# Decoder layer with a routed feed-forward: gate logits of batch 0 before the last out-projection, two copies out of PSUM dropped, fewer spare products, and another order at the end of cross-attention

## What is computed

```python
x = x + xattn(layernorm(x), ctx, bias, mask)      # 16 heads, softmax over the context
x = x + attn(layernorm(x))                        # 16 heads, values clamped
x = x + ffn(layernorm(x))

def ffn(x, gate_w, w1, w2):                       # x: 4 batches, 128 rows, 512 columns
    k = int(2.0 * t / 8)                          # 32 rows for each expert of each batch
    scores = jnp.einsum('ntd,de->nte', x, gate_w)
    probs = jax.nn.softmax(scores, axis=-1)
    probs = jnp.transpose(probs, (0, 2, 1))
    g, m = jax.lax.top_k(probs, k)
    xin = jax.vmap(lambda xb, mb: xb[mb])(x, m)
    h = jax.nn.gelu(jnp.einsum('nekd,edf->nekf', xin, w1))
    h = jnp.einsum('nekf,efd->nekd', h, w2)
    weighted = g[..., None] * h                   # added back to the rows that were chosen
```

## Time and profile before

| | |
|---|---|
| median of 3 runs | 452.39 us |
| lowest and highest | 452.37 and 452.97 us |
| the profiled execution's own time | 454.42 us |
| its span, first to last instruction | 452.7 us |
| mean granted clock of PE | 0.990 |
| PE busy | 440.6 us, 97% |
| DVE busy | 367.3 us, 81% |
| ACT busy | 302.2 us, 67% |
| share of PE in the chain that ended last | 89% |
| share of DVE in it | 6% |

### The profile page before, as it was taken

One profiled execution on the slowest core, in us unless ns is written; L12 is line 12 of the kernel. 1 busy time (PEld: TensorE's weight loads), 2 busy tenths in 40 slices (PEclk: granted clock), 3 DMA queues, 4 the chain that ended last, 5 costly groups with the idle time before them and its releaser, 6 DMA issues.

```text
span 452.7 us, 9864 instructions
## 1 busy us (share of the span) xinstructions
PE 440.6 (97%) x3428; PEld 365.8 (81%) x3428; DVE 367.3 (81%) x516; ACT 302.2 (67%) x622; POOL 87.0 (19%) x111
## 2 busy tenths in 40 slices
PE   8999999999998999999999999999999999999995
PEld 3888888888887789878888787878788787878795
DVE  6889777777779876668978989888989898998972
ACT  4637666666666643667274878787777878777852
POOL 7100000000000122000133250505041230505002
PEclk9999999999999999999979999999999999999999
DMA  7980000000000921800000499999999999998002
GB/s 263 381 295 26 25 23 23 23 23 23 23 26 21 340 89 66 262 19 3 1 0 1 168 387 386 385 387 387 385 332 350 351 307 349 312 376 304 28 1 93
DMA packets 43105, 82.02 MB, mean 181 GB/s; under 512 B 2632, under 2 KB 3784, under 8 KB 43080
## 3 DMA queue, kind: packets, MB, share of 16 engines
q1 hardware_dynamic: 41816, 81.09, 51.0%
q10 hardware_dynamic: 1264, 0.59, 0.5%
HBM read 80.57 MB, written 1.10 MB: 180 GB/s over the span
## 4 chain that ended last, share of the span: by engine, by line
PE 89%; DVE 6%; DMA 1%; issue 1%; ACT 1%; DVEq 0%; POOL 0%; SPq 0%
PE po L1699 19%; PE pk L1699 11%; PE pv L1699 10%; PE pk L1306 8%; PE pv L1316 6%; PE ps L1335 5%; PE ps L1415 3%; PE pv L1335 3%; PE po L1725 3%; PE ps L1460 3%; PE po L1428 2%; PE ps L1408 2%; PE po L1335 2%; DMA x_s<-in_x 1%; PE pk L1335 1%
## 5 line engine op out<-in xcount | busy, mean ns | idle before, releaser
L1242 DVE TENSOR_TENSOR w_lo<-att_w,w_hi 128x2048 fp32r<-128x2048 f32 x60 | 138.0, 2309 | 21.3 <-ACT w_hi L705 21.3
L705 ACT CAST w_hi<-att_w 128x2048 fp32r<-128x2048 f32 x60 | 115.1, 1918 | 15.5 <-PE po L1699 15.5
L488 ACT ACTIVATE big_a<-ps,negm 128x128 f32<-128x128 f32 x176 | 62.2, 394 | 0.0
L1699 PE MATMUL po<-w_hi,ht_hi 128*128 128x512 f32 (+1 forms) x128 | 50.0, 391 | 0.0
L1699 PE MATMUL po<-w_hi,ht_lo 128*128 128x512 f32 (+1 forms) x128 | 48.6, 380 | 0.0
L1699 PE MATMUL po<-w_lo,ht_hi 128*128 128x512 f32 (+1 forms) x128 | 48.6, 380 | 0.0
L1306 PE MATMUL pk<-ctx_s,att_w 128*128 128x128 f32 x352 | 42.1, 278 | 0.0
L1306 PEld LDWEIGHTS pk<-ctx_s,att_w 128*128 128x128 f32 x352 | 40.2, 192 | 1.9 <-issue 1.8
L488 ACT ACTIVATION_READ_ACCUMULATOR big_a<-ps,negm 128x1 f32 x176 | 41.1, 233 | 0.0
L908 DVE TENSOR_REDUCE mc<-ps 128x8 f32<-128x1024 f32 x22 | 26.9, 1221 | 10.0 <-PE ps L1408 9.9
L1699 PEld LDWEIGHTS po<-w_hi,ht_lo 128*128 128x128 f32 x128 | 24.0, 188 | 5.0
(11 more groups left out here) (348 smaller groups left out, 1027.0 us busy)
## 6 DMA issues: line engine op xcount, KB each, us to landing
att_w<-in_w SPq DMA_DIRECT2D x64, 1024.0 KB, 7.2
ctx_s<-in_ctx_t SPq DMA_DIRECT2D x11, 256.0 KB, 2.7
x_s<-in_x SPq DMA_DIRECT2D x4, 256.0 KB, 4.0
att_w<-in_wk SPq DMA_DIRECT2D x1, 1024.0 KB, 8.0
att_w<-in_wq SPq DMA_DIRECT2D x1, 1024.0 KB, 10.4
att_w<-in_wv SPq DMA_DIRECT2D x1, 1024.0 KB, 11.9
att_w<-in_sv SPq DMA_DIRECT2D x1, 1024.0 KB, 14.6
att_w<-in_wo SPq DMA_DIRECT2D x1, 1024.0 KB, 14.8
```

What stands on the lines that cost most here:

```text
L488: ins = a.activation(big_a[:, h], ps[:, c, g * P:(g + 1) * P], ACT.Exp, bias=negm[:, h:h + 1], accum_out=sums[:, h:h + 1])
L705: a.copy(w_hi[:, i % SLOTS], att_w[:, i]).then_inc(hi_ok, 1)
L1242: v.tensor_tensor(w_lo[:, i % SLOTS], att_w[:, i], w_hi[:, i % SLOTS], ALU.subtract).then_inc(lo_ok, 1)
L1699: ins = mm(dst, l, r, start=start and i == 0, stop=i == len(terms) - 1, skip_group_check=True)
```

## The change

Three places in the gate and one in cross-attention:

- `gate_project(0)` moves from behind `turn_gate(2)` to ahead of `out_project(3)`.
- `keep_busy(5, 4)` becomes `keep_busy(3, 4)`.
- The first round of top-k reads the probabilities in `pv`; the copy to `prob_t` is gone. The comparison that makes `onehot` reads the slots in `pk`; the copy to `slot_t` is gone. Since the third group of the gather writes `pk`, PE waits for the second half of `onehot` ahead of it.
- In the step before the last chunk PE runs scores, `turn_batch(1, 0)`, `v_project(t + 1, 3)`, value product, instead of `v_project(t + 1, 3)`, scores, `turn_batch(1, 0)`, value product.

```diff
@@ vector engine, top-k
             dve.wait_ge(pt_g, 1)
-            link(v.tensor_copy(prob_t, pv[0:B * E, 0:T]))
-            src = prob_t
+            src = pv[0:B * E, 0:T]
             for r in range(CAP // 8):
...
             dve.wait_ge(slot_mm, 1)
-            link(v.tensor_copy(slot_t[:], pk[:, 0:B * E]))
...
-                v.tensor_tensor(onehot[:, now].rearrange("p b e s -> p (b e) s"), slot_t[:, rows].unsqueeze(2).broadcast_to([P, 2 * E, CAP]),
+                v.tensor_tensor(onehot[:, now].rearrange("p b e s -> p (b e) s"), pk[:, rows].unsqueeze(2).broadcast_to([P, 2 * E, CAP]),
@@ tensor engine, chunk
-                v_project(t + 1, 3)
-                scores(t + 1)
                 if at_end:
+                    scores(t + 1)
                     turn_batch(1, 0)
+                    v_project(t + 1, 3)
+                else:
+                    v_project(t + 1, 3)
+                    scores(t + 1)
                 values(t)
@@ tensor engine, gate
             out_project(2)
+            gate_project(0)
             out_project(3)
             turn_gate(1)
             turn_gate(2)
-            gate_project(0)
             turn_gate(3)
...
-            keep_busy(5, 4)
+            keep_busy(3, 4)
...
+                if c == 2:
+                    pe.wait_ge(onehot_ok, 2)
```

More of the change, by code:

```diff
@@ L93, in decoder_layer @@
         top8 = sb("top8", [B * E, 8])
-        slot_t = sb("slot_t", [P, B * E])
         iota_s = sb("iota_s", [P, CAP])
@@ L143, in decoder_layer @@
         rounded = sb("rounded", [P, B, D], BF16)
-        prob_t = ctx_s[0:B * E, 0]
         work = ctx_s[0:B * E, 1:3]
```

## The result

| | before | changed |
|---|---|---|
| median | 452.97 us (7 executions) | 455.53 us (7) |
| lowest and highest | 452.37 and 454.45 | 453.82 and 456.38 |
| ratio, with 95% interval | | 1.0043 (1.0028 to 1.0057) |
| profiled execution: own time, span | 454.42, 452.7 | 455.53, 453.8 |
| its mean granted clock | 0.990 | 0.990 |

The change makes the kernel slower by 0.43%, about 1.9 us (the means of the seven executions differ by 2.0, the medians by 2.6). The forecast was +0.2 us.

The account below looks back on a forecast made before the run. PE, busy for 97% of the span, was taken as the bound; cross-attention 0, gate to `onehot` +0.16 and PSUM reads +0.03 gave +0.19, so median 452.39 became 452.6 us, with range 451.2 to 453.3.

Parts of the forecast that it names:

- Cross-attention's end: Last value projection moved behind the scores: value product 0.70 later, absorbed by later waits; cost 0, bounds 0 and +0.7.
- Rival D: Cross-attention's end costs something: the 0.24 slack fails (453.2) or the clock drops there too (455); chance 0.05.
- The order in the gate: Batch 0's logits ahead of the last out-projection: batch 3's logits 0.43 later, bounds 0 and +0.79.
- Rival B: In the gate the clock does not fall, so `onehot` comes earlier: 451.4; chance 0.27.
- The step from there to `onehot`: Gate, batch 3's logits onward: half-rate logits +0.75, partly regained in the 15 spares, `onehot` +0.16; with PSUM reads +0.19.
- The copies: Top-k and slots in the gate read PSUM directly: three reads on DVE, taken +0.03, bounds 0 and 0.1.
- Without the copy 4.34: DVE from start of top-k to the end of batch 3's low part: 4.34 in place of 4.65.
- the 0.31: Time the probabilities' copy held back top-k's first round; its gain was forecast to be hidden by PE's spares.
- Taken +0.03: Forecast cost of three DVE reads from PSUM in the gate, +0.01 each; PE's new wait taken as 0.
- I count everything as the shift of `onehot`: Claim that the experts pass a shift of `onehot` (241.17 before) to the end at full size.
- Two spares fewer: Three spare products in place of five ahead of the probabilities' transpose: gains 0 to 0.1 alone, taken as 0.
- rival C: Gate clock falls and returns later, with two spares gone and PE idle: `onehot` +2.0, time 454.4; chance 0.12.

Follow-up runs that it names:

- attn_only: Kernel before with only the end of cross-attention reordered (scores, transpose, last value projection, value product): median 453.64 us, ratio 1.0004.
- after_keep5: Changed kernel with the unused slots' tensor still laid out and five spare products again in place of three: median 453.40 us, ratio 1.0002.
- order_only: Kernel before with only the gate's order changed, batch 0's logits ahead of the last out-projection: median 453.59 us, ratio 1.0003.
- psum_keep: Kernel before with the two reads from PSUM in place of the copies, slots' tensor still laid out so no address moves: median 453.28 us, ratio 1.0003.
- psum_only: Kernel before with only the two reads from PSUM in place of the copies, PE's wait, and both copies' tensors gone: median 453.91 us, ratio 1.0018.
- pad128: Kernel before, same instructions, with an unused tensor of 128 bytes a partition laid out behind the slots' copy: median 454.55 us, ratio 1.0030.
- after_keep: Changed kernel with the unused slots' tensor still laid out, so addresses are those of the kernel before: median 454.13 us, ratio 1.0017.
- spares_only: Kernel before with only three spare products in place of five ahead of the probabilities' transpose: median 454.01 us, ratio 1.0008.
- expert_pad128: Kernel before with 128 unused bytes right ahead of the experts' operands, moving these and the tensors behind them: median 454.62 us, ratio 1.0031.

## Why the prediction was wrong

**Cross-attention's end: right.** Scores that can't start earlier, the wait moved to PE (0.77, forecast 1.0), a value product 0.69 later counted from the scores (forecast 0.70), absorbed by a wait for DVE. `attn_only` has 1.0004 (0.9991 to 1.0017). Rival D did not come. Of its 12 executions 7 were long, against 35 of 130; `after_keep5` has the same order and had 2 of 12, so this is not laid to the order, and not excluded either.

**The order in the gate: right, and small.** DVE's second half at 228.92 with a wait for PE, the logits of batch 3 0.50 later (forecast 0.43). `order_only` has 1.0003. Rival B, no fall, fell: the clock fell in every profile.

**The step from there to `onehot`: the number right (+0.17, forecast +0.19), by luck.** The sum let the clock fall and return at the moments of the one profile, so that all eight matmuls of batch 3's logits ran at half rate, the first of the 15 spares stood at 236.20 and the clock was full from 238.86. In the trace the clock fell 0.75 later, at 232.78. The eight matmuls took 1.19 in place of 1.73, the probabilities were ready only 0.27 later than before (235.45 and 235.18, the end of DVE's last row for them) and the first of the 15 stood at 235.56, 0.64 ahead of the forecast. But the clock also returned 0.75 later, at 239.61, and the 15 spares took about 0.65 longer than forecast. The two errors cancel in the transpose at 241.05. The second execution of the changed kernel had `onehot` at 241.82. And all of it was worked out from a long execution: in a short one, the more frequent kind in the kernel before, DVE and not the spares ends last.

**The copies: the reads right, their worth not, and wrong in what goes with them.** DVE reads PSUM nearly as fast as SBUF here: MAX8 took 0.29 from `pv` and 0.28 from `ctx_s`. The measurement decides against the Trainium skill's table ("VectorE: DVE Perf Modes", TRN2 errata), as the prediction had taken it. "Without the copy 4.34" was wrong: DVE took 4.80, since its first operation for the slots ended with POOL's piece and not earlier. So in the long execution that the sum was made from the 0.31 was hidden twice, by POOL and by the spares, and in the short kind POOL still takes it. `psum_keep`, of the short kind, took 4.73 from the start of top-k to `onehot`, and the kernel before, of the same kind, 4.80 with both copies. Its ratio (1.0003) shows no gain; its short executions, 452.83 against 453.13 on average, leave room for a small one.

What cost the time is something else. The prediction priced this part as two copies on DVE, three reads and a wait, "Taken +0.03". The edit also removes a tensor, and that moved the operands of self-attention and of the experts by 128 bytes. The steps that failed are this one and the sentence "I count everything as the shift of `onehot`". The second holds for what the gate hands on; it took for granted that what stands ahead of it and behind it goes at its old pace. In its place stand 0.2 in self-attention, seven rounds of +0.11 and +0.24 from the eighth on, +1.2 in the trace. In measured times it is 1.2 (`psum_only` against `psum_keep`) and 1.3 (`pad128`) between short executions, and 1.5 by the ratios (changed against `after_keep`, which ran in different groups).

**Two spares fewer, "Taken: 0": wrong.** The reasoning was made inside one execution, where three spares end before the probabilities are ready. The step put at nothing is the one that rival C names, with a chance of 0.12: that fewer spares ahead of the transpose let the clock return later. It came at a smaller size than its +2.0, as it changes how often an execution is long: 8 of 12 in `spares_only` and in `after_keep`, against 35 of 130 before and 2 of 12 in `after_keep5`. What it costs is less sure: `spares_only` gives +0.4 with an interval that includes no effect, `after_keep` against `after_keep5` +0.7. An idle PE, which rival C gives as one reason, did not separate the two kinds (above); why fewer spares have this effect stays open. The sum had assumed the clock's fall and return as in the one profile; that one was of the rarer kind, and slower than the three timed executions (454.42, median 452.39), which the table of times showed.

**The sum as it should have been**: the place of the operands 1.2, two spares 0.4 to 0.7, the orders and the reads together 0.1 (`after_keep5`, not told from none): 1.7 to 2.0, against 1.9 and 2.3 measured. Of the difference of 2.9 between the forecast 452.6 and the measured 455.53 the rest is no effect of the change: the median of three executions of the kernel before, 452.39, lay below the medians of later groups (452.97 to 453.50), and the changed kernel's median lies above its mean of 455.26.

## What to carry to other kernels

An edit that adds or removes an SBUF tensor moves everything laid out behind it: compare the pace of all untouched stages, ahead of the edit as well as behind it, before explaining a difference by the stage that was edited, and keep the freed bytes laid out when one thing is to be tested. Where several executions of a kernel are shown, see first which kind the profiled one is of; a sum made inside one execution can't price what changes how often each kind comes, and a sum that comes out right is checked at its steps in between. Filler work that seems to end early may still change how often the clock stays low for long. Taking a copy off one engine pays only if no other engine holds it up behind that, here the filler on PE and the work on POOL.

## What the runs showed of the hardware

Products of 512 columns from fp32r operands ran at 232.9 ns from start to start in the experts, and at 234.1 with the operands 128 bytes further on or back (changed kernel, `psum_only`, `pad128`, `expert_pad128`); 256 bytes change nothing and 64 nearly nothing (rounds of 24.98). Self-attention took 57.00 to 57.03 from the scores of cross-attention's last chunk to the row L1331 or L1335 shown with the result, where its operands had moved by 128 bytes (four profiles), and 56.82 to 56.87 in the other twelve. DVE's first operation for the slots (32x128) took 0.21 to 0.67 and never ended ahead of POOL's piece. And one and the same program has executions with 3.41 and with 6.83 us at 0.50 in the gate; the place of the fall is not tied to an instruction (232.03 and 232.57 in two executions of the kernel before, 232.78 and 234.21 in two of the changed one). What decides between the two lengths is open: with three spares ahead of the transpose the long one is frequent, but both lengths came behind a PE that was busy throughout and behind one that had idled.
